# A selective scan in units of 512 columns, two by two, and a last batch in two token halves

## The chip, the cores and the metric

The kernel runs on one core of a Trainium2 chip. The metric is the device time of one launch in microseconds; smaller is better. The engines of the core named here are PE (TensorE, matmuls), DVE (VectorE), ACT (ScalarE), POOL (GpSimd) and SP (SyncE, whose queue issues all the DMAs). Each runs its own list of instructions in order, and they wait for each other through semaphores. SBUF is the on-chip memory; PSUM is the memory that PE writes to, 8 banks of 512 fp32 columns on 128 partitions.

## What is computed

Eight batches of 1024 tokens with 256 channels go through one block: an adaptive layer norm, a selective scan (16 states for each channel), a residual, a second adaptive layer norm, a mixture of experts (8 experts of 256 x 256, the best two by a softmax gate), and a residual. Cut to what matters:

```python
h = _layernorm(x) * (1 + ca) + sa                 # ca, sa, ga ... from silu(c) @ wmod, one set a batch
x_dbl = einsum('bld,ed->ble', h, W_x)             # 64 + 16 + 16 columns: dt_raw, B_sel, C_sel
dt = softplus(einsum('blr,dr->bld', dt_raw, W_dt) + b_dt)
A_bar = exp(dt[..., None] * A)                    # (8, 1024, 256, 16)
dB_u = (dt * h)[..., None] * B_sel[:, :, None, :]
state[l] = A_bar[l] * state[l - 1] + dB_u[l]      # along the 1024 tokens
y = einsum('bldn,bln->bld', state, C_sel)
x = x + ga * (y + h * D_param)
h = _layernorm(x) * (1 + cb) + sb
probs = softmax(h @ Wg);  gates = top2(probs) / sum(top2(probs))
x = x + gb * sum_k gates[k] * (h @ We[k] + be[k])
```

## The kernel before

**Units.** The 256 x 16 pairs of channel and state of a batch are laid out as 32 tiles of 128 partitions (32 channels x 4 states), with the 1024 tokens along the columns. Such a tile is a unit, `u = 0 ... 255` over the eight batches; `unit(u)` gives its batch, its half `hf` of the channels, its group of four states `q` and its 32 channels `j`. Four units with the same `hf` and `q` make a group, and eight groups a batch. For each unit:
- ACT (`decay`, L644) writes `av = exp(A * dt)` into a ring of `AS = 3` slots.
- PE (`spread_b`, L486) spreads B over the partitions once for each group, into the PSUM banks BQ and BQ + 1.
- DVE (`times_b`, L847) multiplies that by `dt * h` into the banks BP and BP + 1: the product. Then DVE (`scan`, L854) runs the recurrence over the 1024 columns, `h = av * h + product`, into a ring of `HS = 8` slots.
- POOL (`times_c`, L977) multiplies two units at once by C, in place. PE (`sums`, L505) sums over the states of a group with eight matmuls (each shows as two records in the trace) into the banks Y and Y + 1.

There is one pair of product banks, so the product of a unit waits for the scan of the unit before it (`s_scan`), and the scan waits for its own product (`s_bm`). `dd` holds `dt` and `dt * h` spread over the partitions; SP fills it by DMA, 16 pieces for `dt` and 16 for `dt * h` for each half batch, and a piece may be overwritten when the last exponential (or product) of the half batch has read it.

**The rest.** While batch b is scanned, the norm, the projections `wx`, `dl` and `C` of batch b + 1 are made, and the tail of batch b - 1: `zs` (L866, DVE: y times gate plus the skip term), `z` (L581, PE: transposes), `zX` (L876, DVE: residual), the second norm, the transposes L525, the logits (L555 to L564) and the softmax with the best two (`soft`, `top`: some 17 small instructions on DVE), the gates to DRAM (`gw`) and back as a broadcast (`gl`, L460), `xg` (L1010, POOL: activations times gate), the experts `f` (L601, PE, with the bias L609), and `o`, `oX` (L570 on PE, L881 on DVE), the last residual. For the last batch this tail is made in two halves of 512 tokens, called A and B, after its scans.

**The order.** It is written out by hand. `schedule()` gives each step a time from the table `AT` (in units from the start of the batch), sorts all steps by it, and each engine runs its steps in that order. So the table decides the place of an instruction in its engine's list, and the semaphores decide when it starts.

Of the kernel before, what the change touches and what calls it, by code (L numbers as in the profile page):

```python
# [14 lines left out]
UB = 2 * NQ * NJ  # L15
TOTAL = NB * UB
LAST = NB - 1
HS, AS, XG, GL = 8, 3, 2, 2
# [31 lines left out]
def before(b, t, put):  # L50
# [19 lines left out]
    for hf in range(2):  # L70
        for c in range(2):
            s = t + AT["dl1" if hf else "dl0"] + AT["dls"] * c
            put(s, "dl", b, hf, c)
            put(s + AT["rdl"], "read", "dl", b, hf, c)
            if in_bank(b, hf):
                put(s + AT["dt"], "dt", b, hf, c)
        if not in_bank(b, hf):
            put(s + AT["sp"], "sp", b, hf)
            put(s + AT["dt"], "dt", b, hf)
        s = t + 16 * hf  # L80
        for j in range(NJ):
            put(s + AT["ddt"] + AT["ddts"] * j, "ddt", 2 * b + hf, j)
            put(s + AT["ddu"] + AT["ddus"] * j, "ddu", 2 * b + hf, j)
# [7 lines left out]
def beside(b, t, put):  # L91

    for i in range(UB):
        for n in ("exp", "mul", "scan"):
            put(t + i + AT[n], n, UB * b + i)
        if i % 2 or alone(UB * b + i):
            put(t + i + AT["ch"], "ch", UB * b + i)
    for i in range(2 * NQ):
        put(t + 4 * i + AT["Bs"], "Bs", 2 * NQ * b + i)
        put(t + 4 * i + AT["y"], "y", 2 * NQ * b + i)  # L100
    for hf in range(2):
        put(t + 16 * hf + 16 + AT["zs"], "zs", b, hf)
# [57 lines left out]
def schedule():  # L160
# [29 lines left out]
def unit(u):  # L190
    b, r = divmod(u, UB)
    return b, r // 16, r // 4 % 4, r % 4


def expert_bank(b, c):

    return FB if b < LAST or c % 3 == 0 else Y + c - 1


class Bank:  # L200
# [17 lines left out]
    def ring(self, s):  # L218
# [5 lines left out]
        if s[:3] == ("xT", 1, LAST) or s[0] in ("lg", "lT", "gT", "o") and s[1] == LAST:  # L224
# [3 lines left out]
def adaln_block(nc, x, A_log, WxT, WdtT, b_dt, D_par, Wg, We, be, cT, wmod, out):  # L228
# [3 lines left out]
    with ExitStack() as ctx:  # L232
# [10 lines left out]

        XN = sb("XN", [P, BLK, D])
# [9 lines left out]
        av = sb("av", [P, AS, L])  # L254
# [31 lines left out]
        iw = sb("iw", [P, 1, E])  # L286

# [757 lines left out]
```

## Time and profile before

| | us |
|---|---|
| median of 3 runs | 1198.14 (1197.16 to 1199.06) |
| the profiled execution: its own time | 1198.99 |
| its span, from the first to the last instruction | 1197.1 |
| mean granted TensorE clock | 0.864 of full speed |
| PE busy | 943.7 (79%) |
| DVE busy | 1006.6 (84%) |
| ACT busy | 703.3 (59%) |
| POOL busy | 924.4 (77%) |

The busy time of an engine is the sum of its instructions' time without overlaps. It doesn't say what an engine waits for, nor what one instruction costs in a row of others: for this, starts have to be compared. The span has a head of some 50 us without scans, the eight batches of scans, and a stretch of some 110 us after the last scan.

### The profile page before, as it was taken

The numbers are of one execution on the slowest core, as the hardware profiler recorded it, in microseconds if no ns is written. First come the engines' busy times: TensorE is split into PE (matmuls) and PEld (weight loads), VectorE is DVE, ScalarE is ACT, GpSimd is POOL, SyncE is SP. The second block draws the span as 40 slices with busy tenths as digits, with TensorE's granted clock in tenths as the row PEclk, the third lists the DMA queues.
The fourth block names the chain that finished last, engine by engine and source line by source line (L and its number), as shares of the span: only waits on it lengthen the run. The fifth ranks groups of instructions, "written<-read, shape, count | busy, mean of one in ns | idle before, by whom it ended". The sixth has DMA issues, their size and how long they took to land. (4 is left out here: it accounts for less than half of the span.)

```text
span 1197.1 us, 13296 instructions
## 1 busy us (share of the span) xinstructions
PE 943.7 (79%) x4235; PEld 598.5 (50%) x4235; DVE 1006.6 (84%) x794; ACT 703.3 (59%) x1331; POOL 924.4 (77%) x306
## 2 busy tenths in 40 slices
PE   6245544589889898789978898788878997889898
PEld 5012111256554565456644565455645665557787
DVE  2399999899999999998999999999999998995110
ACT  4764578556864489557865688557855466331200
POOL 1276666599987899699878999699869998697363
PEclk9565655699997899899989999999989998889999
DMA  5707050545445361737246352647154533621221
GB/s 166 176 16 194 8 135 0 135 133 129 108 97 138 107 171 36 178 106 171 68 98 178 96 142 57 150 122 185 45 129 117 136 97 89 135 69 46 86 74 62
DMA packets 90549, 131.19 MB, mean 110 GB/s; under 512 B 13536, under 2 KB 73512, under 8 KB 90480
## 3 DMA queue, kind: packets, MB, share of 16 engines
q1 hardware_dynamic: 90480, 130.34, 42.6%
q8 instruction: 34, 0.56, 0.2%
q14 instruction: 35, 0.29, 0.1%
HBM read 54.50 MB, written 8.65 MB: 53 GB/s over the span
## 5 line engine op out<-in xcount | busy, mean ns | idle before, releaser
L977 POOL TENSOR_TENSOR h<-h,Cr 128x2048 f32<-128x2048 f32 x129 | 581.9, 4512 | 169.1 <-DVE h L854 109.4
L854 DVE TENSOR_TENSOR_SCAN h<-av,ps 128x1024 f32<-128x1024 f32 x256 | 585.2, 2286 | 25.7 <-ACT av L644 6.5
L601 PE MATMUL ps<-xg,we 128*128 128x256 f32 x2048 | 504.0, 403 | 3.5 <-POOL xg L1010 3.3
L601 PEld LDWEIGHTS ps<-xg,we 128*128 128x128 f32 x2048 | 405.4, 202 | 104.2 <-issue 38.8
L1010 POOL TENSOR_TENSOR xg<-h2T,gbc 128x1024 f32<-128x1024 f32 x128 | 303.7, 2377 | 64.1 <-DMA gbc<-gates 26.2
L847 DVE TENSOR_TENSOR ps<-ps,dd 128x1024 f32<-128x1024 f32 x256 | 315.4, 1232 | 39.3 <-PE ps L486 13.0
L644 ACT ACTIVATE av<-dd,An 128x1024 f32<-128x1024 f32 x256 | 290.5, 1143 | 88.1 <-DVE h L854 77.2
L505 PE MATMUL ps<-h,gam 128*32 128x512 f32 x1024 | 158.0, 745 | 31.0 <-POOL h L977 27.9
L486 PE MATMUL ps<-S,sel 64*128 64x512 f32 x128 | 53.6, 502 | 67.4 <-DVE ps L847 67.3
L732 ACT ACTIVATE z<-ps,md 128x256 f32<-128x256 f32 x64 | 26.7, 469 | 102.4 <-PE ps L609 87.4
L505 PEld LDWEIGHTS ps<-h,gam 128*32 128x32 f32 x1024 | 30.8, 126 | 108.1 <-issue 72.0
L486 PEld LDWEIGHTS ps<-S,sel 64*128 64x128 f32 x128 | 22.1, 214 | 116.8 <-DVE ps L847 97.3
L696 ACT ACTIVATE Cr<-ps 128x512 f32<-128x512 f32 x64 | 37.8, 592 | 63.8 <-PE ps L546 63.6
L881 DVE TENSOR_TENSOR X<-ps,X 128x512 f32<-128x512 f32 x32 | 21.9, 683 | 58.2 <-PE ps L570 58.0
L546 PE MATMUL ps<-S,sel 64*128 64x512 f32 x64 | 33.7, 529 | 37.1 <-ACT Cr L696 36.8
L525 PE MATMUL ps<-identf,XM 128*128 128x128 f32 x128 | 23.7, 319 | 37.4 <-ACT XM L761 30.8
L539 PE MATMUL ps<-rows,wrow 64*128 64x512 f32 x64 | 41.9, 739 | 13.0 <-DVE X L881 9.4
L688 ACT ACTIVATE src<-ps,bd 128x512 f32<-128x512 f32 x30 | 20.5, 683 | 45.8 <-PE ps L539 45.7
L525 PE MATMUL ps<-identf,XN 128*128 128x128 f32 x128 | 28.1, 363 | 21.9 <-DVE X L881 9.8
L660 ACT ACTIVATE hT<-ps,md 128x512 f32<-128x512 f32 x32 | 24.6, 776 | 34.0 <-PE ps L525 33.8
L660 ACT ACTIVATE h2T<-ps,md 128x512 f32<-128x512 f32 x32 | 24.6, 775 | 29.0 <-PE ps L525 25.2
L546 PEld LDWEIGHTS ps<-S,sel 64*128 64x128 f32 x64 | 13.3, 209 | 55.1 <-ACT Cr L696 47.9
(99 smaller groups left out, 743.2 us busy)
## 6 DMA issues: line engine op xcount, KB each, us to landing
dd<-src SPq DMA_DIRECT2D x512, 128.0 KB, 2.5
gbc<-gates SPq DMA_DIRECT2D x128, 256.0 KB, 3.7
X<-in_x SPq DMA_DIRECT2D x8, 1024.0 KB, 9.3
out<-X SPq DMA_DIRECT2D x32, 256.0 KB, 3.6
XN<-in_x SPq DMA_DIRECT2D x7, 1024.0 KB, 7.5
we<-in_We SPq DMA_DIRECT2D x2, 1024.0 KB, 8.5
XN<-in_x SPq DMA_DIRECT2D x2, 512.0 KB, 4.8
Cr<-in_wmod SPq DMA_DIRECT2D x1, 1024.0 KB, 5.2
```

Of the source, the lines that this page charges most:

```text
L486: e = pe.matmul(ps[:, BQ + c], sel[R:P, q], S[R:P, b % 2, c * CH:(c + 1) * CH], start=True, stop=True)
L505: e = pe.matmul(ps[32 * j:32 * j + 32, Y + c], gam[:, b % 2, 2 * j + hf], h[:, (4 * g + j) % HS, c * CH:(c + 1) * CH], start=(q == 0), sto ...
L525: e = pe.transpose(bk[:, q * P:(q + 1) * P], (XM[:, q] if w else XN[:, 4 * c + q])[:, hf * P:(hf + 1) * P], identf[:])
L539: e = pe.matmul(bk, wdt[:, hf * P:(hf + 1) * P], dtr[:, c * CH:(c + 1) * CH], start=True, stop=True)
L546: e = pe.matmul(bk, sel[R:P, NQ + q], S[R:P, b % 2, c * CH:(c + 1) * CH], start=True, stop=True)
L601: e = pe.matmul(bk[:, m * 256:(m + 1) * 256], we[:, hf, 2 * ep + e2, m * P:(m + 1) * P], xg[:, i % XG, e2, hf], start=(ep == e2 == m == hf ...
L644: act.activation(av[:, u % AS], dd[:, j, 0], ACT.Exp, scale=An[:, 0, i:i + 1]).then_inc(s_a, 1)
L660: release(act.activation(dst, mb(s), ACT.Identity, bias=md[:, 6 * w + hf, b:b + 1], scale=md[:, 6 * w + 2 + hf, b:b + 1]), s)
L847: dve.tensor_tensor(wide(BP), wide(BQ), dd[:, j, 1], ALU.mult).then_inc(s_bm, 1)
L854: dve.tensor_tensor_scan(h[:, u % HS], av[:, u % AS], wide(BP), 0.0, ALU.mult, ALU.add).then_inc(s_scan, 1)
L977: pool.tensor_tensor(hu, hu, Cr[:, q:q + 1].to_broadcast([P, n, L]), ALU.mult).then_inc(s_ch, n)
L1010: pool.tensor_tensor(xg[:, i % XG], h2T[:, :, 256 * c:256 * c + 256].unsqueeze(1).to_broadcast([P, 2, 2, 256]), gbc[:, i % GL].unsqueeze(2 ...
```

## The change

- `UB` is 64: a unit now has 512 columns (`CH`), one half `c` of the tokens. Up to the seventh batch the order within a group is j = 0, 1 of the first half, j = 0, 1 of the second half, then the same for j = 2, 3. Two products stand together, then their two scans.
- The products of even and odd units lie in different banks (`product(u)`). A product waits for the scan two units before (`u - 1` scans done), not for the one before.
- The scan of the second half starts from the last column of the first half's (`start`, a pointer into `h`).
- Each of the two banks of spread B is filled and released by itself.
- `av` has 6 slots of 512 columns; `h` is as large as before; POOL still multiplies 2048 columns at once.
- The last batch runs all its units for the first 512 tokens and then all for the second. POOL keeps the last column of each first-half scan in a new tile `kept` before it multiplies in place, and the second half starts from it. `dl`, softplus, `dd`, the sums, `zs` and `z` of that batch go by token halves too, and tail A can start while half B is scanned.
- The table `AT` is a new one.

```diff
-UB = 2 * NQ * NJ
+UB = 4 * NQ * NJ
+LAST = NB - 1
+FULL = LAST * UB
 TOTAL = NB * UB
-LAST = NB - 1
-HS, AS, XG, GL = 8, 3, 2, 2
+T = UB // 2
+HS, AS, XG, GL = 8, 6, 2, 2
...
-AT = dict(exp=0.54, mul=0.01, scan=0.63, ch=7.93, Bs=0.65, y=7.82, stat0=-2.76, stat0s=0.51, rstd0=1.18,
+AT = dict(exp=0.31, mul=0.01, scan=0.7, ch=7.43, Bs=0.67, Bss=0.56, y=7.81, stat0=-3.62, stat0s=0.59,
...
+    for r in range(UB):
+        put(t + r / 2 + AT["exp" + k], "exp", u0 + r)
+        put(t + r // 2 + AT["mul" + k] + 0.05 * (r % 2), "mul", u0 + r)
+        put(t + r // 2 + AT["scan" + k] + 0.05 * (r % 2), "scan", u0 + r)
+        if r % 4 == 3 or alone(u0 + r):
+            put(t + r / 2 + AT["ch" + k], "ch", u0 + r)
...
 def unit(u):
+
     b, r = divmod(u, UB)
-    return b, r // 16, r // 4 % 4, r % 4
+    if b < LAST:
+        return b, r // 32, r // 8 % 4, r // 4 % 2 * 2 + r % 2, r // 2 % 2
+    return b, r // 16 % 2, r // 4 % 4, r % 4, r // 32
...
+        def product(u):
+            return ps[:, BP + u % 2]
+
+        def spread(u):
+            return ps[:, BQ + (unit(u)[4] if u < FULL else u // 4 % 2)]
...
+def spread_free(n):
+
+    if n < spreads(LAST):
+        return 4 * n - 2 * (n % 2) - 2
+    return FULL + 4 * (n - spreads(LAST) - 1) if n > spreads(LAST) else FULL - 2
...
-                if g:
-                    pe.wait_ge(s_bm, 4 * g)
-                for c in range(2):
-                    e = pe.matmul(ps[:, BQ + c], sel[R:P, q],
-                                  S[R:P, b % 2, c * CH:(c + 1) * CH], start=True, stop=True)
-                e.then_inc(s_br, 1)
+                if spread_free(n) > 0:
+                    pe.wait_ge(s_bm, spread_free(n))
+                pe.matmul(spread(u), sel[R:P, q], S[R:P, b % 2, c * CH:(c + 1) * CH], start=True, stop=True).then_inc(s_br, 1)
...
-                act.activation(av[:, u % AS], dd[:, j, 0], ACT.Exp, scale=An[:, 0, i:i + 1]).then_inc(s_a, 1)
+                act.activation(av[:, u % AS], step_of(u, 0), ACT.Exp, scale=An[:, 0, i:i + 1]).then_inc(s_a, 1)
...
             def times_b(u):
-                b, hf, q, j = unit(u)
-                if q == 0:
-                    dve.wait_ge(s_ddu[j], 64 * (2 * b + hf + 1))
-                if j == 0:
-                    dve.wait_ge(s_br, u // 4 + 1)
-                if u:
-                    dve.wait_ge(s_scan, u)
-                dve.tensor_tensor(wide(BP), wide(BQ), dd[:, j, 1], ALU.mult).then_inc(s_bm, 1)
+
+                landed(dve, u, s_ddu)
+                dve.wait_ge(s_br, spread_of(u) + 1)
+                if u >= 2:
+                    dve.wait_ge(s_scan, u - 1)
+                dve.tensor_tensor(product(u), spread(u), step_of(u, 1), ALU.mult).then_inc(s_bm, 1)
 
             def scan(u):
-                if u >= HS:
-                    dve.wait_ge(s_y, (u - HS) // 4 + 1)
+
+                b, hf, q, j, c = unit(u)
+                start = 0.0
+                if h_owner(u) >= 0:
+                    dve.wait_ge(s_y, h_owner(u) + 1)
+                if c and b < LAST:
+                    dve.wait_ge(s_scan, u - 1)
+                    start = state(u - 2)[:, CH - 1:CH]
+                elif c:
+                    i = 16 * hf + 4 * q + j
+                    if j == 0:
+                        dve.wait_ge(s_kept, i // 4 + 1)
+                    start = kept[:, i:i + 1]
                 dve.wait_ge(s_bm, u + 1)
                 dve.wait_ge(s_a, u + 1)
-                dve.tensor_tensor_scan(h[:, u % HS], av[:, u % AS], wide(BP), 0.0, ALU.mult, ALU.add).then_inc(s_scan, 1)
+                dve.tensor_tensor_scan(state(u), av[:, u % AS], product(u), start, ALU.mult, ALU.add).then_inc(s_scan, 1)
...
+                if b == LAST and half == 0:
+                    i = 16 * hf + 4 * q
+                    pool.tensor_copy(kept[:, i:i + 4].unsqueeze(2), hu[:, :, CH - 1:CH]).then_inc(s_kept, 1)
+                    pool.wait_ge(s_kept, i // 4 + 1)
+                pool.tensor_tensor(hu, hu, cu, ALU.mult).then_inc(s_ch, n)
```

On DVE, in the middle of the kernel, products (L847), scans (L854) and between them the steps of the tail stand before like this; the names in brackets are the semaphores that a row waits for (`s_scan`: scans done, `s_bm`: products done, `s_br`: B spread, `s_a`: exponential done, `s_y`: a slot of `h` free):

```order
L847 TENSOR_TENSOR ps<-ps,dd 128x1024 [waits s_scan]
L854 SCALAR_TENSOR_TENSOR h<-av,ps 128x1024 [waits s_a,s_bm,s_y]
L847 TENSOR_TENSOR ps<-ps,dd 128x1024 [waits s_scan,s_br]
L854 SCALAR_TENSOR_TENSOR h<-av,ps 128x1024 [waits s_a,s_bm,s_y]
L847 TENSOR_TENSOR ps<-ps,dd 128x1024 [waits s_scan]
L881 TENSOR_TENSOR X<-ps,X 128x512 [waits s_pm]
L854 SCALAR_TENSOR_TENSOR h<-av,ps 128x1024 [waits s_a,s_bm,s_y]
```

And now, at such a place, with the product at L957, the scan at L975 (`h<-av,h,ps` is a second half, with its pointer into `h`) and L1006 for L881:

```order
L957 TENSOR_TENSOR ps<-ps,dd 128x512 [waits s_scan,s_br] x2
L975 SCALAR_TENSOR_TENSOR h<-av,h,ps 128x512 [waits s_bm,s_a,s_scan,s_y] x2
L957 TENSOR_TENSOR ps<-ps,dd 128x512 [waits s_scan,s_br] x2
L1006 TENSOR_TENSOR X<-ps,X 128x512 [waits s_pm]
L975 SCALAR_TENSOR_TENSOR h<-av,ps 128x512 [waits s_a,s_bm,s_y] x2
```

Product and scan alternated; now two products are followed by the two scans.

On PE, from the last sum (L505) of the last batch on, the order before is this (L601 experts, L609 bias, L570 `o`, L581 `z`, L525 transposes of the second norm, L555 to L564 logits and gates):

```order
L505 MATMUL ps<-h,gam 32x512 x8
L570 MATMUL ps<-identf,z 128x128 x4
L601 MATMUL ps<-xg,we 128x256 x8
L581 MATMUL ps<-identf,hT 128x128 x8
L601 MATMUL ps<-xg,we 128x256 x8
L609 MATMUL ps<-rows,wrow 128x256 x2
L581 MATMUL ps<-identf,hT 128x128 x8
L601 MATMUL ps<-xg,we 128x256 x8
L525 MATMUL ps<-identf,XM 128x128 x8
L601 MATMUL ps<-xg,we 128x256 x8
L555 MATMUL ps<-h2T,wgp 32x256 x4
```

And now (L615 sum, L711 experts, L719 bias, L680 `o`, L691 `z`, L635 transposes, L665 and L670 logits):

```order
L711 MATMUL ps<-xg,we 128x256 x8
L635 MATMUL ps<-identf,XM 128x128 x4
L615 MATMUL ps<-h,gam 32x512 x4
L635 MATMUL ps<-identf,XM 128x128 x4
L711 MATMUL ps<-xg,we 128x256 x8
L665 MATMUL ps<-h2T,wgp 32x256 x4
L615 MATMUL ps<-h,gam 32x512 x4
L670 MATMUL ps<-identf,gam 128x128 x2
L711 MATMUL ps<-xg,we 128x256 x8
L719 MATMUL ps<-rows,wrow 128x256 x2
L680 MATMUL ps<-identf,z 128x128 x4
L691 MATMUL ps<-identf,hT 128x128 x8
```

The transposes and the logits of tail A stood behind the last sum and stand before it now; behind it the list holds 168 expert matmuls, where it held 176, and one batch of eight `z` transposes, where it held two.

## Rows read from the trace of the kernel before

**Rows 1.** The page's first part: busy us (share of the span) x instructions, by engine.
```profile
PE 943.7 (79%) x4235; PEld 598.5 (50%) x4235; DVE 1006.6 (84%) x794; ACT 703.3 (59%) x1331; POOL 924.4 (77%) x306
```

**Rows 2.** Windows view: stretch, length, busy PE, PEld, DVE, ACT, POOL, clock, DMA.
```profile
280.00:410.00 130.00, 111.97 (x505) 70.34 (x498) 121.95 (x91) 87.35 (x170) 112.84 (x35) 0.90 0.48 122
```

**Rows 3.** The page's costliest groups: busy, mean ns | idle before, releaser.
```profile
L854 DVE TENSOR_TENSOR_SCAN h<-av,ps 128x1024 f32<-128x1024 f32 x256 | 585.2, 2286 | 25.7 <-ACT av L644 6.5
...
L847 DVE TENSOR_TENSOR ps<-ps,dd 128x1024 f32<-128x1024 f32 x256 | 315.4, 1232 | 39.3 <-PE ps L486 13.0
L644 ACT ACTIVATE av<-dd,An 128x1024 f32<-128x1024 f32 x256 | 290.5, 1143 | 88.1 <-DVE h L854 77.2
...
L688 ACT ACTIVATE src<-ps,bd 128x512 f32<-128x512 f32 x30 | 20.5, 683 | 45.8 <-PE ps L539 45.7
```

**Rows 4.** DVE's timeline in the middle: start us, duration us, instruction.
```profile
440.26 0.68 DVE L881 TENSOR_TENSOR X<-ps,X 128x512 f32<-128x512 f32 x1
440.86 2.28 DVE L854 TENSOR_TENSOR_SCAN h<-av,ps 128x1024 f32<-128x1024 f32 x1
443.05 1.26 DVE L866 SCALAR_TENSOR_TENSOR hT<-hT,Dga,ps 128x1024 f32<-128x1024 f32 x1
444.22 1.23 DVE L847 TENSOR_TENSOR ps<-ps,dd 128x1024 f32<-128x1024 f32 x1
445.54 2.29 DVE L854 TENSOR_TENSOR_SCAN h<-av,ps 128x1024 f32<-128x1024 f32 x1
447.93 1.23 DVE L847 TENSOR_TENSOR ps<-ps,dd 128x1024 f32<-128x1024 f32 x1
449.07 1.22 DVE L876 TENSOR_TENSOR X<-ps,X 128x1024 f32<-128x1024 f32 x1
450.20 2.28 DVE L854 TENSOR_TENSOR_SCAN h<-av,ps 128x1024 f32<-128x1024 f32 x1
```

**Rows 5.** DVE's timeline at other places (in brackets: idle before, releaser).
```profile
44.54 1.23 DVE L847 TENSOR_TENSOR ps<-ps,dd 128x1024 f32<-128x1024 f32 x1 [12.15 <-DMA dd<-src]
50.25 2.29 DVE L854 TENSOR_TENSOR_SCAN h<-av,ps 128x1024 f32<-128x1024 f32 x1 [4.48 <-ACT av L644]
52.64 1.23 DVE L847 TENSOR_TENSOR ps<-ps,dd 128x1024 f32<-128x1024 f32 x1
...
299.77 2.29 DVE L854 TENSOR_TENSOR_SCAN h<-av,ps 128x1024 f32<-128x1024 f32 x1
...
512.10 0.70 DVE L861 TENSOR_TENSOR S<-ps,S 32x512 fp32r<-32x512 f32 x1
512.82 2.29 DVE L854 TENSOR_TENSOR_SCAN h<-av,ps 128x1024 f32<-128x1024 f32 x1
...
957.78 2.29 DVE L854 TENSOR_TENSOR_SCAN h<-av,ps 128x1024 f32<-128x1024 f32 x1
...
1084.04 1.23 DVE L847 TENSOR_TENSOR ps<-ps,dd 128x1024 f32<-128x1024 f32 x1
1085.36 2.29 DVE L854 TENSOR_TENSOR_SCAN h<-av,ps 128x1024 f32<-128x1024 f32 x1
```

**Rows 6.** PE's timeline from the last sum on, three of its rows.
```profile
1092.03 1.92 PE L505 MATMUL ps<-h,gam 128*32 128x512 f32 x16 [0.89 <-POOL h L977]
...
1118.66 3.62 PE L601 MATMUL ps<-xg,we 128*128 128x256 f32 x16
...
1190.31 1.13 PE L609 MATMUL ps<-rows,wrow 8*128 8x256 f32 x4
```

**Rows 7.** Waits of DVE: who <- for whom: us in total, times, longest.
```profile
DVE ps L847 <- PE ps L486: 13.0, 12, 2.0
```

**Rows 8.** Waits of POOL, the two for transfers and for experts.
```profile
POOL xg L1010 <- DMA gbc<-gates: 26.2, 6, 10.5
POOL xg L1010 <- PE ps L601: 25.1, 15, 3.3
```

**Rows 9.** Waits of SP's queue, the longest in total.
```profile
SPq L460 <- POOL xg L1010: 365.0, 78, 8.7
```

More of the change, by code:

```diff
@@ L75, in before @@
             if in_bank(b, hf):
[L76 to L83, printed above, removed]
+                put(s + AT["dt"], "dt", b, w, i)
+        if not in_bank(b, w):
+            put(s + AT["sp"], "sp", b, w)
+            put(s + AT["dt"], "dt", b, w)
+        for part in range(2 if (b, w) == (LAST, 1) else 1):
+            s = t + (T + T // 4 * part if (b, w) == (LAST, 1) else T // 2 * w)
+            k = "L" if (b, w) == (LAST, 1) else ""
+            for j in range(NJ):
+                put(s + AT["ddt" + k] + AT["ddts" + k] * j, "ddt", 2 * b + w, j, part)
+                put(s + AT["ddu" + k] + AT["ddus" + k] * j, "ddu", 2 * b + w, j, part)
     for q in range(NQ):
@@ L91, in beside @@
 def beside(b, t, put):
[L93 to L102, printed above, removed]
-    put(t + AT["ldx2"], "ldx2", b)
+    put(t + AT["ldx2"], "ldx2", b)
+    u0, k = UB * b, "L" if b == LAST else ""
+    for r in range(UB):
[4 more added lines that the diff above has]
+            put(t + r / 2 + AT["ch" + k], "ch", u0 + r)
+    if b == LAST:
+        for i in range(UB // 4):
+            put(t + 2 * i + AT["BsL"], "Bs", spreads(b) + i)
+            put(t + 2 * i + AT["yL"], "y", groups(b) + i)
+        for i in range(4):
+            put(t + 8 * i + 8 + AT[f"zsL{i}"], "zs", b, i % 2, i // 2)
+    else:
+        for i in range(2 * NQ):
+            for c in range(2):
+                put(t + 4 * i + AT["Bs"] + AT["Bss"] * c, "Bs", spreads(b) + 2 * i + c)
+            put(t + 4 * i + AT["y"], "y", groups(b) + i)
+        for hf in range(2):
+            put(t + 16 * hf + 16 + AT["zs"], "zs", b, hf)
 def after(b, t, put):
@@ L109, in after @@
         s = t + AT["z"] + AT["zd"] * kp
+        if b == LAST:
+            s = t + T // 2 * (kp + 1) + AT[f"zL{kp}"]
         put(s, "z", b, kp)
-        put(s + AT["zX"], "zX", b, kp)
+        put(s + AT[f"zXL{kp}" if b == LAST else "zX"], "zX", b, kp)
     if b < LAST - 1:
@@ L170, in schedule @@
     for b in range(NB):
-        before(b, UB * (b - 1), put)
-        beside(b, UB * b, put)
-        after(b, UB * (b + 1), put)
+        before(b, T * (b - 1), put)
+        beside(b, T * b, put)
+        after(b, T * (b + (b < LAST)), put)
     return [step for _, step in sorted(at, key=lambda p: p[0])]
@@ L242, in wide, with state, step_of, landed @@
             return ps[:, bk:bk + 2].rearrange("p a c -> p (a c)")
+        def state(u):
+            at = h_place(u)
+            return h[:].rearrange("p s l -> p (s l)")[:, at * CH:(at + 1) * CH]
+        def product(u):
+            return ps[:, BP + u % 2]
+        def spread(u):
+            return ps[:, BQ + (unit(u)[4] if u < FULL else u // 4 % 2)]
+        def step_of(u, kind):
+            _, hf, _, j, c = unit(u)
+            part = c if u < FULL else hf
+            return dd[:, j, kind, part * CH:(part + 1) * CH]
+        def landed(eng, u, sems):
+            b, hf, q, j, c = unit(u)
+            if q == 0:
+                H = 2 * b + (hf if b < LAST else c)
+                eng.wait_ge(sems[j], 64 * (H + 2 if b == LAST and c and hf else H + 1))
         XN = sb("XN", [P, BLK, D])
```

205 lines of the change are left out of this document (128 added, 77 removed).

## The prediction, written before the changed kernel was run

> **What bounds the kernel now.** I read the engines' busy time first. No engine is full over the whole span: DVE has 1006.6 us of 1197.1 and PE 943.7 [rows 1]. But in a stage in which all the work runs together, DVE is busy 121.95 us of 130 while PE has 111.97, POOL 112.84 and ACT 87.35 [rows 2]. The groups by line say what DVE does there: 256 scans of 2286 ns and 256 products of 1232 ns, 900.6 of its 1006.6 us [rows 3]. The DVE timeline comes next, because durations hide what matters here. Measured from start to start, an instruction costs something else than its duration, and that depends on who follows it [rows 4]:
> - product, then its own scan: 444.22 to 445.54, 1.32 us; product, then an instruction that doesn't need it: 447.93 to 449.07, 1.14 us.
> - scan, then the next product (which overwrites the bank that the scan reads): 445.54 to 447.93, 2.39 us (2.32 where the product has one wait less); scan, then an instruction that doesn't need it: 440.86 to 443.05, 2.19 us.
> So an instruction starts some 0.08 us ahead of its predecessor's end if they are independent, and 0.02 to 0.10 us behind it if they are not. With one pair of product banks every unit pays both: 3.64 to 3.71 us for work that would take 1.14 + 2.19 = 3.33. In the whole timeline 208 products are followed at once by their scan (from 52.64 to 1084.04) and 206 scans at once by the next product; the rest has something else in between. From the first scan of the third batch at 299.77 to that of the last at 957.78 are five batches, 131.6 us each; the first scan starts at 50.25 and the last at 1085.36 [rows 5]. The last look is at the end: from the last sum at 1092.03 to the last bias matmul at 1190.31 PE runs nearly without a break [rows 6]; that stretch is work of PE, not waits.
>
> **Part 1: units of 512 columns, in pairs (order of DVE: P0 P1 S0 S1).** Removed: the dependent steps. No product stands any more directly ahead of its scan, and the product that overwrites a bank comes one instruction later than the scan that reads it, since there are two banks. P1's 0.6 us lies between P0 and S0, and S1's 1.1 us between S0 and the next P0; both are longer than the 0.10 us by which a dependent start came late. Gain: 208 x (1.32 - 1.14) = 37 us and 206 x (2.35 - 2.20) = 31 us (2.35 is the mean of the 206, nearly all of them 2.32 or 2.39), together 68 us.
> Added: twice as many instructions. The fixed part of a step: 512 columns of L881 take 0.60 us to the next start (440.26 to 440.86), 1024 columns of L876 take 1.13 (449.07 to 450.20), so 512 columns are 0.53 and 0.07 is fixed [rows 4]. A product of 1024 at 1.14 becomes two of 0.60: +0.06. The scan of 512 is in no row. If its fixed part is the 0.07 of the others, it takes (2.20 - 0.07) / 2 + 0.07 = 1.135, two of them 2.27: +0.07. Bounds: +0, if nothing of the 2.20 is fixed, and +0.17, if the whole 0.17 by which its duration of 2.286 exceeds twice 1.06 (the columns' own 0.53, at two passes) has to be paid each time. I take +0.07, since three instruction kinds in rows 4 overlap their neighbours alike. 256 x (0.06 + 0.07) = 33 us. Half of the scans now take their start from the scan two before, through a pointer; L866 with its pointer steps 1.17 (443.05 to 444.22) where L876 without one steps 1.13: 128 x 0.04 = 5 us. Net of part 1: 68 - 33 - 5 = 30 us less.
>
> The Trainium skill speaks against this. "VectorE: DVE Perf Modes", section "The DRAIN you can't avoid", says that after each DVE operation the next waits until the pipe is empty, whether there is a semaphore or not, and its rules say to keep the number of operations small. By that the 68 us wouldn't come and only the cost would; rows 4 show 1.32 against 1.14 behind the same product, so this trace doesn't agree. "Vector Engine (DVE) Microarchitecture Reference", section "Measured stream behaviour on trn2", gives some 75 ns fixed per instruction after overlap; with it the 33 us would be 256 x 2 x 0.075 = 38, near what the rows give.
>
> **Part 2: finer waits around it.** Each bank of spread B is refilled for itself. Before, PE refilled both after the fourth product, beside one scan of 2.3 us; DVE waited 13.0 us for it in all [rows 7]. Now some 5.8 us of DVE work (two scans, two products, two scans) stand between the release of a bank and its next use, so I take 10 of the 13 us as gained, 0 to 13. ACT makes twice as many exponentials. One of 1024 columns lasts 1143 ns, and another activation with a pointer operand lasts 683 at 512 columns (L688), so two for one cost at most 0.22 us more [rows 3], 7 us on 87 of 130 us a batch. The ring av holds as many columns as before. DVE's own work hides this; without that cover it would be 7 x 8 = 56 us. POOL multiplies by C in the same pieces of 2048 elements, and the ring h is as deep as before.
> What is late next is POOL: 112.84 us busy of 130, and beside that it waited 26.2 us for gbc and 25.1 for PE over the kernel [rows 8], some 8 us a batch. 121 us of need against a new period of some 127 leaves room, but not for every order of its queue. I put 4 us of new waits into the sum (0 to 20).
>
> **Part 3: last batch in two token halves.** On DVE the residual add of the first half (1.1 us) and its norm statistics (1.8 us, four bn_stats and four bn_aggr) move from the idle time after the scans to between them, +3 us; the eight small copies `kept` go to POOL. After the last scan: it ended at 1087.65 [rows 5], but two multiplications of 1024 columns were then left for POOL, and the sum that waited for them came at 1092.03 [rows 6]. Now the last four are of 512 columns and the last sum is four matmuls: 2 us less. On PE, behind the last sum stand 168 expert matmuls instead of 176 (two records each, 3.62 us for 16 records [rows 6]: 3.5 us), half of the transposes of hT and XM and one of two logits products, 3 us. That work doesn't vanish; it moves to the scan phase, where PE has 18 us idle of 130. Against it the router's chain for the second half (gates, write, broadcast, first product) has fewer matmuls to hide behind, 1 to 2 us. Net 5 us less (0 to 10).
>
> **Sum.** 30 + 10 - 4 - 3 + 2 + 5 = 40 us. The head (first scan at 50.25) stays within a us: its first scan waits for ACT, which has one exponential of half the size ahead of it. The profiled execution took 1198.99 us (span 1197.1), 0.85 above the median of 1198.14: 1198.99 - 40 = 1159, or 1158 beside the median. As I counted the 4 us of new waits from the low side, I say **1160**.
>
> **Rivals.**
> - *POOL or PE becomes the bound.* They keep a period of about 129 instead of 127, in-order waits included. For it: 112 and 113 us busy of 130, and SP's queue waited 365 us for POOL's products [rows 9], so the three are coupled. Against: both idle some 18 us of 130, part of it because they wait for DVE. Half of parts 1 and 2 is lost: 1180.
> - *Nothing overlaps.* The short scans behave like L861, the one instruction with 0.72 us to the next start at a duration of 0.70 (512.10 to 512.82). Then a product of 512 steps 0.73 and a scan 1.25: 3.96 a unit of 1024 against 3.67, 256 x 0.29 = 74 us more, less the 14 of the rest: 1258. Against: L861 is also the only one that works on partitions 96 to 127; all others in rows 4 overlap. It turns slower as soon as a pair of steps costs over 1.84 us. The Trainium skill's rule named above, from "The DRAIN you can't avoid", would have it so.
> - *dd comes late.* Of each pair of pieces of dd one is now free half a unit (1.8 us) later and the other needed half a unit earlier; the queue of SP in front of them can be held for up to 8.7 us by POOL [rows 9]. If each of the 15 reloads makes DVE wait 3 us, 45 us are lost: 1205. It decides against the change from 2.7 us a reload. Against: before, DVE waited for dd only once, at the start [rows 5].
> - *The time moves into the tail.* PE must do the same 944 us of work; if it doesn't keep up in the scan phase, it ends as late as before but for part 3: 1193.
>
> **Chances.** Forecast 0.61; POOL or PE 0.19; no overlap 0.07; dd late 0.08; tail 0.05. No change is within 0.2% (2.4 us), about what can be told apart here. Faster 0.84 (forecast, POOL or PE, most of the tail), same 0.03, slower 0.13. Range: all unknowns at their good end (fixed cost of the scan 0: 18 us; waits 13; no new waits; tail 10) give 1130, of which not all come together: low 1138. High 1190, which takes in the POOL rival and leaves out the slow ones.
>
> **What would show it.** In the DVE timeline: product to product and product to scan 0.60 to 0.62 us, scan to next 1.13 to 1.18; a unit of two pairs within 3.5 us; batches of 126 to 128 us. No wait of L957 for spread B beyond 3 us in all. The last scan ends near 1055, the last sum some 4 us later, and from there some 98 us to the end. Wrong if a short scan steps over 1.25 us (overlap or fixed cost), if waits of DVE for av, dd or h's slots grow beyond 10 us (rings), or if the batches are shorter but the stretch after the last scan longer (tail).

## The result, and the profile after

| | before | changed | ratio |
|---|---|---|---|
| median of 4 runs, us | 1197.65 | 1162.24 | 0.9702 (95%: 0.969 to 0.9714) |
| the profiled execution, us | 1198.99 | 1162.86 | |
| its span, us | 1197.1 | 1160.6 | |
| first scan starts | 50.25 | 46.94 | 3.3 earlier |
| from there to the end of the last scan | 1037.4 | 1010.65 | 26.8 shorter |
| from there to the end of the span | 109.45 | 103.0 | 6.4 shorter |

The last three rows add up to the 36.5 us of span. The forecast was 1160.

Busy time by engine, against [rows 1], and the middle of the kernel in the windows view, against [rows 2] (stretch, length, busy PE, PEld, DVE, ACT, POOL, clock, DMA share, GB/s):

```profile
PE 933.8 (80%) x4235; PEld 583.3 (50%) x4235; DVE 1005.8 (87%) x1308; ACT 750.4 (65%) x1587; POOL 925.8 (80%) x316
```

```profile
410.00:540.00 130.00, 113.55 (x544) 71.08 (x542) 127.39 (x160) 98.36 (x218) 118.34 (x37) 0.95 0.50 128
```

DVE's busy time is what it was (1005.8 against 1006.6 us) although it has 514 instructions more. In the middle it is busy 127.4 of 130 us; [rows 2] has 122.0, and the kernel before in these same 130 us 123.8. Most of the gaps are gone. The groups that answer to [rows 3]:

```profile
L754 ACT ACTIVATE av<-dd,An 128x512 f32<-128x512 f32 x512 | 348.2, 713 | 94.4 <-DVE h L975 70.2
...
L957 DVE TENSOR_TENSOR ps<-ps,dd 128x512 f32<-128x512 f32 x512 | 326.9, 683 | 18.5 <-DMA dd<-src 12.9
L975 DVE TENSOR_TENSOR_SCAN h<-av,ps 128x512 f32<-128x512 f32 x256 | 299.0, 1205 | 2.7 <-ACT av L754 2.4
L975 DVE TENSOR_TENSOR_SCAN h<-av,h,ps 128x512 f32<-128x512 f32 x224 | 273.8, 1264 | 0.5
```

DVE's timeline at the start of the fourth batch (start, duration, instruction; "x2" are two instructions in one row), against [rows 4]:

```profile
419.63 2.33 DVE L975 TENSOR_TENSOR_SCAN h<-av,ps 128x512 f32<-128x512 f32 x2
421.87 0.68 DVE L1006 TENSOR_TENSOR X<-ps,X 128x512 f32<-128x512 f32 x1
422.45 1.30 DVE L957 TENSOR_TENSOR ps<-ps,dd 128x512 f32<-128x512 f32 x2
423.64 2.45 DVE L975 TENSOR_TENSOR_SCAN h<-av,h,ps 128x512 f32<-128x512 f32 x2
426.00 1.28 DVE L957 TENSOR_TENSOR ps<-ps,dd 128x512 f32<-128x512 f32 x2
427.18 1.22 DVE L975 TENSOR_TENSOR_SCAN h<-av,ps 128x512 f32<-128x512 f32 x1
430.30 1.28 DVE L991 SCALAR_TENSOR_TENSOR hT<-hT,Dga,ps 128x1024 f32<-128x1024 f32 x1 [1.90 <-PE ps L615]
```

Start to start, two products take 1.18 (426.00 to 427.18), two scans 2.24 without the pointer (419.63 to 421.87) and 2.36 with it (423.64 to 426.00). The work of 1024 columns is 3.42 or 3.54 us, where [rows 4] had 3.64 to 3.71. In these rows every instruction starts ahead of its predecessor's end, except where another engine is late, as at 430.30. DVE's waits, whole kernel (who waits for whom: us, times, longest), against [rows 7], and PE's wait for the same banks in the other direction:

```profile
DVE hT L991 <- PE ps L615: 12.4, 6, 3.5
...
DVE ps L957 <- PE ps L595: 5.5, 2, 4.0
```

```profile
PE ps L595 <- DVE ps L957: 10.8, 6, 2.9
```

The wait for spread B fell from 13.0 to 5.5 us, and a new one of 12.4 stands beside it: `zs` waits for the sum of a batch's last group. Counting stops of more than 0.15 us, DVE idles 25.2 us between its first and its last scan, and 22.2 before; the short gaps behind dependent steps are not in these sums (with them it is 30.3, and 59.0 before). The batches (the third and the last start here; the last row ends the scans), against [rows 5]:

```profile
292.74 1.21 DVE L975 TENSOR_TENSOR_SCAN h<-av,ps 128x512 f32<-128x512 f32 x1
...
930.10 2.32 DVE L975 TENSOR_TENSOR_SCAN h<-av,ps 128x512 f32<-128x512 f32 x2
...
1055.15 2.44 DVE L975 TENSOR_TENSOR_SCAN h<-av,kept,ps 128x512 f32<-128x512 f32 x2
```

Five batches take 637.4 us, 127.5 each (131.6 before). At the end, PE's last sum and last bias matmul, against [rows 6], and what POOL did ahead of that sum:

```profile
1065.10 0.62 PE L615 MATMUL ps<-h,gam 128*32 128x512 f32 x2
...
1065.52 1.03 PE L615 MATMUL ps<-h,gam 128*32 128x512 f32 x6
...
1154.30 1.13 PE L719 MATMUL ps<-rows,wrow 8*128 8x256 f32 x4
```

```profile
1058.56 2.37 POOL L1150 TENSOR_TENSOR xg<-h2T,gbc 128x1024 f32<-128x1024 f32 x1
1060.88 3.71 POOL L1111 TENSOR_TENSOR h<-h,Cr 128x512 f32<-128x512 f32 x3
```

The last sum has eight records, two from 1065.10 and six from 1065.52. It starts 7.5 us behind the last scan (4.4 before) and 95.5 us ahead of the end (105.1 before).

### The profile page after: what moved, and what is told of

It is laid out like the page before. It is cut to its first block and busy times, and to the rows that moved or that the text cites. A ratio compares the mean times of both kernels' runs of the same rounds, so it can differ in the third digit from the quotient of the medians.

```text
span 1160.6 us, 15054 instructions
## 1 busy us (share of the span) xinstructions
PE 933.8 (80%) x4235; PEld 583.3 (50%) x4235; DVE 1005.8 (87%) x1308; ACT 750.4 (65%) x1587; POOL 925.8 (80%) x316
## 5 line engine op out<-in xcount | busy, mean ns | idle before, releaser
L1111 POOL TENSOR_TENSOR h<-h,Cr 128x2048 f32<-128x2048 f32 (+1 forms) x131 | 582.3, 4447 | 107.4 <-DVE h L975 84.4
L711 PE MATMUL ps<-xg,we 128*128 128x256 f32 x2048 | 491.1, 396 | 9.7 <-POOL xg L1150 7.5
L711 PEld LDWEIGHTS ps<-xg,we 128*128 128x128 f32 x2048 | 397.2, 198 | 105.3 <-issue 34.9
L754 ACT ACTIVATE av<-dd,An 128x512 f32<-128x512 f32 x512 | 348.2, 713 | 94.4 <-DVE h L975 70.2
L957 DVE TENSOR_TENSOR ps<-ps,dd 128x512 f32<-128x512 f32 x512 | 326.9, 683 | 18.5 <-DMA dd<-src 12.9
L975 DVE TENSOR_TENSOR_SCAN h<-av,ps 128x512 f32<-128x512 f32 x256 | 299.0, 1205 | 2.7 <-ACT av L754 2.4
L975 DVE TENSOR_TENSOR_SCAN h<-av,h,ps 128x512 f32<-128x512 f32 x224 | 273.8, 1264 | 0.5
L615 PE MATMUL ps<-h,gam 128*32 128x512 f32 x1024 | 160.4, 747 | 53.1 <-POOL h L1111 46.7
L615 PEld LDWEIGHTS ps<-h,gam 128*32 128x32 f32 x1024 | 29.9, 124 | 126.2 <-issue 70.6
L1006 DVE TENSOR_TENSOR X<-ps,X 128x512 f32<-128x512 f32 x32 | 21.7, 678 | 65.5 <-PE ps L680 65.4
L595 PE MATMUL ps<-S,sel 64*128 64x512 f32 x128 | 65.1, 527 | 11.2 <-DVE ps L957 10.8
L1132 POOL TENSOR_TENSOR src<-src,hT 128x1024 f32<-128x1024 f32 (+1 forms) x15 | 33.3, 2220 | 25.7 <-ACT src L789 25.7
L595 PEld LDWEIGHTS ps<-S,sel 64*128 64x128 f32 x128 | 24.8, 202 | 56.4 <-DVE ps L957 26.9
L656 PE MATMUL ps<-S,sel 64*128 64x512 f32 x64 | 32.3, 507 | 22.7 <-ACT Cr L808 13.4
L770 ACT ACTIVATE hT<-ps,md 128x512 f32<-128x512 f32 x32 | 24.6, 773 | 35.7 <-PE ps L635 35.5
L635 PE MATMUL ps<-identf,XM 128*128 128x128 f32 x128 | 22.0, 300 | 29.5 <-ACT XM L873 20.9
L680 PE MATMUL ps<-identf,z 128*128 128x128 f32 x128 | 21.7, 294 | 26.5 <-ACT Cr L808 11.9
L635 PE MATMUL ps<-identf,XN 128*128 128x128 f32 x128 | 27.0, 352 | 19.7 <-ACT hT L770 18.1
```

Source lines behind the costliest of these rows:

```text
L595: pe.matmul(spread(u), sel[R:P, q], S[R:P, b % 2, c * CH:(c + 1) * CH], start=True, stop=True).then_inc(s_br, 1)
L615: e = pe.matmul(ps[32 * j:32 * j + 32, Y + (c if b < LAST else hf)], gam[:, b % 2, 2 * j + hf], state(u), start=(q == 0), stop=(q == NQ - 1))
L635: e = pe.transpose(bk[:, q * P:(q + 1) * P], (XM[:, q] if w else XN[:, 4 * c + q])[:, hf * P:(hf + 1) * P], identf[:])
L711: e = pe.matmul(bk[:, m * 256:(m + 1) * 256], we[:, hf, 2 * ep + e2, m * P:(m + 1) * P], xg[:, i % XG, e2, hf], start=(ep == e2 == m == hf ...
L754: act.activation(av[:, u % AS], step_of(u, 0), ACT.Exp, scale=An[:, 0, i:i + 1]).then_inc(s_a, 1)
L957: dve.tensor_tensor(product(u), spread(u), step_of(u, 1), ALU.mult).then_inc(s_bm, 1)
```

## The experiments

All times are medians; the kernel before, run beside them, had 1197 to 1198. `after` is the changed kernel. The theory throughout: DVE's steps set the period, a dependent step is what costs, and the rest hides. The rivals: POOL and PE hold the period, or the time only changes its place. No run tries the new table `AT` by itself: runs 1, 2, 5 and 8 take one part out of `after` and leave its table in place (run 5 has the old entries for its tail), and runs 3 and 4 keep the table of the kernel before (run 4 moves products and scans alone).

**1. The pairing undone** (order P0 S0 P1 S1, all else as in `after`).

```diff
+    for u in range(1, TOTAL, 2):
+        plan.remove(("scan", u - 1))
+        plan.insert(plan.index(("mul", u)), ("scan", u - 1))
```

> The changed kernel with one thing undone: on DVE the order is P0 S0 P1 S1 instead of P0 P1 S0 S1; units of 512 columns, two product banks, table and waits stay. Theory (the gain is the dependent steps that went away): a product directly ahead of its scan steps about 0.78 us instead of 0.59, some 450 to 500 of the 512 products stand so, +80 to +90 us: 1240 to 1255 us. Rival (the gain comes from two banks, finer waits and the new table, pairing as such does nothing): within 5 us of 1162.

1279.09 us, ratio to before 1.0703 (1.067 to 1.0735). DVE's timeline:

```profile
420.01 0.68 DVE L961 TENSOR_TENSOR ps<-ps,dd 128x512 f32<-128x512 f32 x1
420.78 1.22 DVE L979 TENSOR_TENSOR_SCAN h<-av,ps 128x512 f32<-128x512 f32 x1
421.92 0.67 DVE L961 TENSOR_TENSOR ps<-ps,dd 128x512 f32<-128x512 f32 x1
422.79 1.28 DVE L979 TENSOR_TENSOR_SCAN h<-av,h,ps 128x512 f32<-128x512 f32 x1 [0.20 <-DVE ps L961]
```

A product followed by its own scan steps 0.77 (0.87 if that scan has a pointer) instead of 0.59. Of the 512 products 450 are followed at once by their scan, 216 without and 234 with a pointer: 216 x 0.18 + 234 x 0.28 = 104 us. DVE's other stops grow from 25 to 35 us, and the scans end 113 us later. The order alone turns the change from 3% faster to 7% slower. The direction was expected; the size was too small, since I had carried over the 0.18 for all of them. Why the pointer scan, which has one wait more, starts 0.1 us later still isn't settled: nothing here varies the waits alone.

**2. The pointer left out** (in the first seven batches the second halves start from 0.0; that part of the recurrence is not computed).

```diff
-                    start = state(u - 2)[:, CH - 1:CH]
```

> The changed kernel, but the scans of the second token half of the first seven batches start from 0 and not through a pointer; the carry between the halves is left out there. Theory (DVE bounds, the pointer costs 0.06 us a scan): 224 scans x 0.06 = 13 us less, 1149 us, second-half scans step 1.12 us. Rival (POOL or PE already sets the pace): the steps get shorter but waits of DVE take it back, 1158 to 1162 us.

1157.00 us, 0.9681 (0.9652 to 0.971). 480 scans last 1.20 us; the 32 of the last batch that start from `kept` still last 1.26. The scans' own gain is 224 x 0.06 = 13 us, but the time falls by 5.2, nearer to the rival than to the theory: `zs` waits 14.4 us for its sum (12.4) and DVE idles 29.5 between scans (25.2), so about two fifths of a gain on DVE arrive.

**3. The split alone**, on the kernel before: both products of a unit, then both scans, each half in its own bank, nothing else changed.

```diff
+                for c in range(2):
+                    if u:
+                        dve.wait_ge(s_scan, 2 * (u - 1) + c + 1)
+                    dve.tensor_tensor(ps[:, BP + c], ps[:, BQ + c], dd[:, j, 1, c * CH:(c + 1) * CH], ...)
...
+                    if c:
+                        dve.wait_ge(s_scan, 2 * u + 1)
+                        start = h[:, u % HS, CH - 1:CH]
```

> The kernel before, with its own table and order of units, but product and scan of each unit cut in two halves of 512 columns: P(first) P(second) S(first) S(second), in the two banks it has. Theory: P steps 0.59 twice; S(first) is directly followed by the scan that needs it, 1.23 to 1.30 us; S(second) with its pointer 1.18: 3.59 to 3.66 a unit against 3.64 to 3.71 before, so 0 to 15 us less than before: 1183 to 1198 us. Rival (smaller pieces with a bank each are what helps): like the changed kernel without its last batch, 1165 to 1172 us.

1214.89 us, 1.0183 (1.0137 to 1.0229): slower than before, against the expectation.

```profile
440.62 1.21 DVE L861 TENSOR_TENSOR_SCAN h<-av,ps 128x512 f32<-128x512 f32 x1
441.93 1.28 DVE L861 TENSOR_TENSOR_SCAN h<-av,h,ps 128x512 f32<-128x512 f32 x1
443.13 1.27 DVE L848 TENSOR_TENSOR ps<-ps,dd 128x512 f32<-128x512 f32 x2
444.31 1.21 DVE L861 TENSOR_TENSOR_SCAN h<-av,ps 128x512 f32<-128x512 f32 x1
```

The second scan follows the one whose last column it reads: 1.31 to its start, against 1.12. A unit costs 3.69 (440.62 to 444.31), no less than the 3.64 to 3.71 of [rows 4]. And it pays this every time: the two scans always stand together, 1.32 us from start to start on average, where in the kernel before some 45 of the 256 units had a step of the tail between product and scan and paid less. So a bank for each half is not enough while a scan stands right behind the one that it continues; in `after` three others stand between them (for S2, which continues S0: S1 P2 P3).

**4. Pairs without the split**: units of 1024 columns in the order P0 P1 S0 S1 on the kernel before. PSUM has no room for two such products, so that of every odd unit goes into its slot of `h` in SBUF and is scanned in place.

```diff
+        def product(u):
+            return h[:, u % HS] if u % 2 else wide(BP)
```

> The kernel before with its units of 1024 columns, but in pairs P0 P1 S0 S1: the product of an odd unit is written into its own slot of the ring h in SBUF, and the scan runs in place there, so no PSUM bank is missing. No cut, no pointer. Theory: steps of 1.14 and 2.20, 3.34 us a unit: up to 68 us less than before, 1130 us, if nothing else binds. Rival 1 (POOL or PE sets the pace at some 122 to 124 us a batch): 1140 to 1155 us, with waits of DVE for PE and POOL. Rival 2 (a scan or product with its operands in SBUF is slower or slows POOL, since both work on SBUF): odd scans over 2.29 us or POOL's multiplication over 4.55 us, 1180 us or more.

1327.69 us, 1.1108 (1.1074 to 1.1142). The groups:

```profile
L860 DVE TENSOR_TENSOR_SCAN h<-av,h 128x1024 f32<-128x1024 f32 x128 | 451.7, 3529 | 25.2 <-ACT av L648 25.2
L1016 POOL TENSOR_TENSOR xg<-h2T,gbc 128x1024 f32<-128x1024 f32 x128 | 420.4, 3288 | 58.6 <-PE ps L605 28.4
...
L860 DVE TENSOR_TENSOR_SCAN h<-av,ps 128x1024 f32<-128x1024 f32 x128 | 291.1, 2274 | 1.0 <-ACT av L648 0.5
```

The same scan with both inputs in SBUF lasts 3.53 us on average, and POOL's products slow down with it, 3.29 against 2.38. Neither the place of the data nor scanning in place does this by itself: 15 of these 128 scans run while POOL does nothing and last 2.27 us each, and the other 113 last 3.70 on average, up to 6.19. One of each kind on DVE, and what POOL did beside the second:

```profile
186.04 2.26 DVE L860 TENSOR_TENSOR_SCAN h<-av,h 128x1024 f32<-128x1024 f32 x1
...
431.71 6.18 DVE L860 TENSOR_TENSOR_SCAN h<-av,h 128x1024 f32<-128x1024 f32 x1
```

```profile
431.20 4.54 POOL L983 TENSOR_TENSOR h<-h,Cr 128x2048 f32<-128x2048 f32 x1
435.68 4.38 POOL L1016 TENSOR_TENSOR xg<-h2T,gbc 128x1024 f32<-128x1024 f32 x1
```

The independent steps are as cheap as forecast (product to product 1.14, scan to scan 2.20), and that is of no use: Rival 2 came true. "SBUF — State Buffer", section "Who interferes with whom", of the Trainium skill says that a DVE instruction with two SBUF inputs contends with a GpSimd instruction that reads SBUF; these rows agree.

**5. The last batch in one piece** (its order, its projections and its tail as before, and none of its last units multiplied alone on POOL; batches 0 to 6 as in `after`).

```diff
-FULL = LAST * UB
+SPL = NB
+FULL = SPL * UB
...
-    if b == LAST:
+    if b == SPL:
```

> The changed kernel without its third part: the last batch is scanned like the seven others, with its tail A and B after all scans (the table's entries for A and B are those of the kernel before). Theory (units in pairs give the scan phase, the two halves only 5 to 8 us behind the last scan): scans end within 3 us of the changed kernel's 1057.6, and 1165 to 1172 us in all. Rival (the last batch in halves gives more than a third of the 36 us): 1175 us or more.

1182.38 us, 0.9878 (0.9854 to 0.9902). The scans end at 1056.54, as in `after`, but the span goes on for 121.5 us, which is 18.5 more than `after` and 12 more than before. POOL, then PE:

```profile
1059.37 2.34 POOL L1150 TENSOR_TENSOR xg<-h2T,gbc 128x1024 f32<-128x1024 f32 x1 [2.53 <-PE ps L719]
1061.66 4.52 POOL L1111 TENSOR_TENSOR h<-h,Cr 128x2048 f32<-128x2048 f32 x1
```

```profile
1067.96 1.92 PE L615 MATMUL ps<-h,gam 128*32 128x512 f32 x16
```

POOL's last multiplication by C stands behind an `xg` that waits for PE, and the last sum comes 11.4 us after the last scan. From that sum on PE has 97.65 us of work, as before (97.51), in 110 us. So of the 31.1 us by which the scans end earlier than before, 12 went into the tail here. Against this run, halving the last batch takes 8.5 us of work (89.17 remain) and 6 us of idle time out of PE's tail and brings the sum 3.9 us closer. The tail of this run has the order that was made for the kernel before; how much of the 20 us a better order without halves would keep is not shown.

**6. The head** (the transfer of ga, on which POOL's first `gam` waits, ahead of the second batch's tokens in SP's queue, where it was before).

```diff
-... ga=17.04, ...
+... ga=-0.84, ...
```

> The changed kernel with one entry of its table put back (ga from 17.04 to -0.84): the 16 small transfers of ga stand in SP's queue ahead of the load of the second batch's x again. Theory (that load lets ACT start its norm statistics and so the first exponential earlier): the first scan starts 2 to 3.5 us later than 46.9 us, and the kernel takes 1164 to 1166 us. Rival: the first scan doesn't hang on it, 1162 us.

1160.42 us, 0.9697 (0.9673 to 0.972).

```profile
49.96 1.22 DVE L975 TENSOR_TENSOR_SCAN h<-av,ps 128x512 f32<-128x512 f32 x1
...
59.77 2.33 DVE L975 TENSOR_TENSOR_SCAN h<-av,ps 128x512 f32<-128x512 f32 x2 [2.04 <-ACT av L754]
```

The first scan is 3.0 us later, as expected, and the end isn't: the second batch starts at 167.17 (167.72 in `after`), and the scans end 2.8 us earlier. The first batch has slack, so the 3.3 us of the head in the first table bring nothing by themselves. My own theory, that they count in full, fell.

**7. `zs` one unit of time later** on DVE.

```diff
-... zs=2.72, ...
+... zs=3.72, ...
```

> The changed kernel with zs one unit of 1024 columns later in DVE's list in the first seven batches (zs from 2.72 to 3.72). The changed kernel waits 12.4 us there for PE's sums, which wait for POOL. Theory (DVE bounds and this wait is a matter of place): most of the 12.4 us goes, 1150 to 1156 us. Rival (POOL sets the pace; what DVE doesn't wait for here it waits for elsewhere): 1160 us or more.

1162.24 us, 0.9709 (0.9685 to 0.9733): the same as `after`.

```profile
DVE ps L957 <- PE ps L595: 15.8, 14, 4.8
```

The 12.4 us behind L615 are gone, and the wait for spread B has grown by 10.3. It was no matter of the place in DVE's list: what DVE doesn't wait for here, it waits for elsewhere, and in both places PE is the one that comes late.

**8. Spread B refilled as before**, both banks after the last product of a group.

```diff
-        return 4 * n - 2 * (n % 2) - 2
+        return 4 * (n - n % 2)
```

> The changed kernel, but both banks of spread B are refilled only when all eight products of a group are done (first seven batches). Theory (finer waits were worth the 7 us by which DVE's wait for spread B fell from 13.0 to 5.5): the wait comes back to 10 us or more, 1168 to 1175 us. Rival (that wait was going to be covered anyway): within 2 us of 1162.

1186.24 us, 0.9898 (0.9871 to 0.9926): 24 us slower than `after`, more than the 6 to 13 us that I expected. PE's wait, and DVE's timeline at the same place as above:

```profile
PE ps L595 <- DVE ps L957: 35.7, 20, 3.5
```

```profile
431.82 0.69 DVE L1006 TENSOR_TENSOR X<-ps,X 128x512 f32<-128x512 f32 x1 [3.29 <-PE ps L680]
```

DVE's wait for spread B itself is nearly unchanged (6.5 us). What grew is its wait for `o`, from 2.2 to 22.8 us between the scans: PE stands in front of the refill, and `o` is queued behind. PE waited 67.3 us for these banks before, 35.7 here, and 10.8 in `after`. But the kernel before, in which PE waited longest, lost only 1.6 us to `o` between its scans. So the 24 us are the price of the coarse refill in this order of PE's queue, not of the refill alone.

**9 to 11. One place in PE's queue.** In `after`, POOL has finished the last group at 425.1, and PE takes the sum up at 428.31, after eight expert matmuls. Put ahead of them:

```diff
-            put(t + 4 * i + AT["y"], "y", groups(b) + i)
+            put(t + 4 * i + AT["y"] - 1.4 * (i == 7), "y", groups(b) + i)
```

> The sum of the last group of a batch goes ahead of eight expert matmuls in PE's queue (16 records of the trace, 3.7 to 5.3 us), and nothing else moves. In the changed kernel DVE waits for this sum five times between 290 and 930 us, 11.5 us in all (1.9 each, once 3.5), while POOL had finished the last group 3.2 us before PE took the sum up (425.1 against 428.3). Theory (the 12.4 us of waits are the price of one place in PE's queue): the five waits go, DVE's idle time between the scans falls from 25 to about 14 us, and the time is about 10 us less, 1152. Rival (PE has no time to give: the matmuls that wait behind the sum make something else late, a refill of spread B or a read of C): the waits change their names as they did when the step was moved on DVE, idle time stays at about 25, and the time stays within 2 us of the changed kernel's, 1160 to 1164.

> Both small edits together: the last group's sum ahead of the experts in PE's queue, and the transfer of ga ahead of the second batch's tokens in SP's queue. The second alone was worth 1.8 us. If both are independent, 1150 under the theory that the sum's place costs 10 us, and 1160 under the rival that it costs nothing.

> The changed kernel once more, on the same chip and in the same call as the two edits, as their reference: 1162, within 2 us.

1179.54 us (0.9845, 0.9825 to 0.9866); with the edit of run 6 as well 1178.02 (0.9835, 0.9814 to 0.9856); `after` beside them 1161.96 (0.9703, 0.9682 to 0.9725). Both theories missed: the swap costs 17 us (1179.54 against 1161.96). PE in `after`, and then in this kernel:

```profile
423.06 5.32 PE L711 MATMUL ps<-xg,we 128*128 128x256 f32 x16
428.31 1.92 PE L615 MATMUL ps<-h,gam 128*32 128x512 f32 x16
```

```profile
425.28 3.64 PE L615 MATMUL ps<-h,gam 128*32 128x512 f32 x16 [1.81 <-POOL h L1111]
428.85 4.42 PE L711 MATMUL ps<-xg,we 128*128 128x256 f32 x16
```

The windows view, in `after` and then in this kernel (columns as in [rows 2]):

```profile
420.00:423.00 3.00, 1.49 (x6) 0.78 (x6) 3.00 (x4) 3.00 (x13) 3.00 (x2) 0.99 0.78 217
423.00:426.00 3.00, 3.00 (x8) 2.40 (x8) 3.00 (x4) 3.00 (x8) 3.00 (x2) 0.50 0.93 209
426.00:429.00 3.00, 3.00 (x18) 1.99 (x21) 2.40 (x4) 2.79 (x6) 3.00 (x2) 0.94 0.69 216
```

```profile
420.00:423.00 3.00, 2.15 (x6) 1.28 (x6) 3.00 (x4) 3.00 (x12) 3.00 (x2) 0.51 0.83 219
423.00:426.00 3.00, 1.19 (x5) 0.20 (x8) 3.00 (x4) 3.00 (x7) 3.00 (x2) 0.50 0.99 220
426.00:429.00 3.00, 3.00 (x17) 0.54 (x9) 2.49 (x5) 2.96 (x6) 3.00 (x2) 0.50 0.61 196
```

PE now idles for POOL first. The granted clock is at half (1.2 GHz) here from 420 to 430, and in `after` from 423 to 426, where it slows the experts (5.32 us for 16 records, against 3.72 at 431.22). In this kernel the sum lies within the slow stretch, and its 16 records take 3.64 us instead of 1.92. The clock fell before the wait of 1.81 us began (at 423.5), so that wait didn't bring it down. From 420 to 426 PE was busy for 3.3 us here and for 4.5 in `after`; why the fall comes 3 us earlier is open. Over the five batches the clock is 0.91 on average here and 0.93 in `after`; how much of the 17 us is the clock and how much the order was not separated. The next refill of spread B comes 3.0 us later (437.91 against 434.87), and DVE, which got `zs` 1.3 us earlier, waits 3.51 for it. Its waits for spread B add up to 26.2 us (5.5 before the swap).

No version beat the changed kernel by more than can be told: run 6 is 0.16% below it (the same edit takes 1.5 us off run 9 as well), and run 2 leaves work out.

## Why the prediction was right

1160 against 1162.24, in the range, with the mechanism named as the main one; but several terms were off and cancelled.

- **Dependent steps gone, -68 us.** Right, and shown: steps of 0.59 and 1.12 (1.18 with the pointer) where 0.60 to 0.62 and 1.13 to 1.18 were forecast, and run 1 brings the cost back by the order alone. The rival "Nothing overlaps" is out. (Its 1258 takes 14 us for the rest of the sum; without the 4 us of new waits that is right, with them it is 10, and the rival 1262.) The Trainium skill ("VectorE: DVE Perf Modes", section "The DRAIN you can't avoid") has the next instruction wait for an empty pipe; short scans that start 0.60 us behind the start of a product of 0.68 us don't agree. But the same section adds that an instruction which isn't held starts earlier, which the prediction left out, and the section "Two Vector instructions with no wait between them" gives a rule by start partitions for those that are held. With it, the start 0.03 us late behind the one instruction on partitions 96 to 127 [rows 5] is no surprise.
- **Cutting in two, +33 us.** Measured 20: a pair of products 1.18 against 1.14, a pair of scans 2.24 against 2.20, 256 x 0.08. **The pointer, +5 us**, was mis-sized: I counted 128 such scans, but there are 256 (half of 512), and each costs 0.06, not 0.04: 15 us. Both errors nearly cancel; part 1 is 68 - 20 - 15 = 33 us, forecast 30.
- **Waits, -10 + 4.** Wrong by 9 us: measured +3 on DVE (22.2 to 25.2 us), against -6. The wait for spread B fell by 7.5 to 5.5, above the 3 that the prediction had as its sign, and `zs` took more than that back. The term looked only at DVE's own wait for the refill. Run 8 shows what the finer refill is for: PE no longer stands in front of it, which in this order is worth 24 us, most of it in `o`, an instruction that my sum never named. Two smaller readings were off too: the waits of POOL in [rows 8] are 51.3 us, 6.4 a batch and not 8, and two short exponentials cost 0.28 us more than a long one (2 x 0.713 against 1.143), not at most 0.22. ACT's time stayed hidden.
- **Part 3, +3 on DVE, -2 handover, -5 tail.** The total was right (6.4 us less after the last scan, forecast 7), the parts weren't. The last sum came 3.1 us later relative to the scans instead of 2 earlier, since POOL had an `xg` and three multiplications left and PE 16 records of experts; from it on PE's stretch was 9.6 us shorter. And the 4 us that the sum gives part 3 as a whole (2 + 5 - 3) compare it with the kernel before only: with the last batch in one piece and the old order of its tail, 12 us of the scans' gain are lost in the tail (run 5). The rival "The time moves into the tail" comes true in part without part 3, and by run 5 part 3 is worth up to 20 us behind parts 1 and 2.
- **The head within a us.** It was 3.3 us earlier: the second batch's tokens now come first in SP's queue. (In the runs with this queue the first scan starts between 45.2 and 47.9, and in the two with the transfer of ga put back, at 50.0 and 49.6.) Run 6 shows that this has no worth, so the error did no harm.
- **"POOL or PE becomes the bound"** is half true. Neither is full (118.3 and 113.6 of 130 us), and the batches shrank to 127.5 as forecast; but PE's order holds DVE up. Runs 2, 7 and 9 show it: a gain on DVE arrives by two fifths, a wait taken away comes back under another name, and one sum moved ahead of eight experts costs 17 us over seven batches.
- **dd late** did not happen: between the scans DVE waited for it 0.9 us.

## What to carry to other kernels

Compare starts, not durations: the price of an instruction depends on whether the one ahead of it feeds it. Two independent chains taken in turn (P0 P1 S0 S1) win that back, if a second buffer exists in a memory that nobody else contends for, and if no step reads what the one directly ahead of it wrote. Refill a shared buffer piece by piece for the sake of the in-order queue that does the refilling; what stands behind it was the larger part here (run 8). And when a stage in the middle becomes shorter, look at what the engines still have queued at its end.

## What I had not expected of the hardware

- A DVE step behind the instruction it depends on costs some 0.18 us more, at 512 columns as at 1024 (0.77 against 0.59, 1.32 against 1.14), and 0.28 where the waiting scan also has a pointer and a fourth wait.
- Scan of 512 fp32 columns: 1.205 us, stepping 1.12; with its start through a pointer 1.264 and 1.18.
- Scan of 1024 columns with both inputs in SBUF beside POOL at work: 3.70 us on average, up to 6.19, against 2.27 while POOL is idle, or with one input in PSUM.
- A sum of 16 records took 3.64 us at the halved clock and 1.92 at the full one; the order of PE's queue decided which work fell into the slow stretch, and the stretch was 10 us long in one order and 3 in the other.
